# Attention slots: outputs in slots 0 to 3, keys and queries two by two, x turned in slots 5 and 6

## The reference, cut to what matters

```
x = LN(where(vol > 0.5, x + circuit(x), x + gelu(x@w1+b1)@w2+b2))     # per batch, then scale and shift
q, k, v = x@Wq+bq, x@Wk+bk, x@Wv+bv                                   # 16 heads of 32 columns
p   = softmax(q k^T / sqrt(32) + bias[b, head], masked columns -> 0)  # bias is 8x16x512x512
x   = x + (p v)@Wo + bo                                               # attention
out = h + gelu(h@W1+b1)@W2+b2, h = LN(x)*g2+beta2                     # second FFN
```

## Time and profile before

| What | Value |
|---|---|
| median of 3 runs | 2408.28 us (2406.91 to 2420.22) |
| the profiled execution's own time | 2410.64 us |
| its span, first to last instruction | 2408.8 us |
| mean granted TensorE clock | 0.997 |
| first FFN / attention / second FFN | 798.2 / 887.2 / 723.4 us |
| a middle batch of attention | 110.9 to 111.4 us |

### The profile page before, as it was taken

The page is one execution under the profiler, slowest core; times in us unless marked ns, Lnnn a source line. Parts: engine busy times, 40 slices in busy tenths (PEclk is TensorE's granted clock), DMA queues, the critical chain, the costliest instruction groups (busy, mean ns, idle before and its releaser), DMA issues. The chain is left out here.

```text
span 2408.8 us, 42244 instructions
## 1 busy us (share of the span) xinstructions
PE 2368.5 (98%) x16104; PEld 1896.9 (79%) x16104; DVE 1355.8 (56%) x2749; ACT 1010.2 (42%) x2057; POOL 1018.5 (42%) x829
## 2 busy tenths in 40 slices
PE   9999999999999899999999999998999999999999
PEld 7788888888887677777777777776888888888887
DVE  7354454454457777777777777778443333323332
ACT  6132232231332776767666676767311211111111
POOL 0042241431424896767676776767112112202200
PEclk9999999999999999999999999999999999999999
DMA  7110111101123466565656565574420110110100
GB/s 230 45 44 18 44 35 44 44 17 61 44 80 111 148 192 199 158 209 162 201 163 198 168 200 184 173 209 156 131 71 1 52 52 0 52 52 0 52 35 18
DMA packets 142197, 243.94 MB, mean 101 GB/s; under 512 B 14140, under 2 KB 28620, under 8 KB 142048
## 3 DMA queue, kind: packets, MB, share of 16 engines
q1 hardware_dynamic: 140992, 241.40, 31.3%
q10 hardware_dynamic: 1056, 0.52, 0.1%
HBM read 216.69 MB, written 25.20 MB: 100 GB/s over the span
## 5 line engine op out<-in xcount | busy, mean ns | idle before, releaser
L1251 POOL TENSOR_TENSOR at_bias<-at_bias,at_mask 128x512 f32<-128x512 f32 x512 | 592.7, 1186 | 239.2 <-DMA at_bias<-in_fside_Bx16xSxS 226.7
L647 ACT ACTIVATE L_hid<-bank,L_b1c 128x512 f32<-128x512 f32 x256 | 176.6, 690 | 961.6 <-PE bank L290 961.4
L843 DVE CAST L_hh<-L_hid 128x512 fp32r<-128x512 f32 x256 | 121.7, 475 | 743.2 <-PE bank L970 714.5
L288 PE MATMUL bank<-xth,L_w1h 128*128 128x512 f32 x1024 | 402.7, 393 | 0.5 <-DVE L_w1l L714 0.5
L289 PE MATMUL bank<-xth,L_w1l 128*128 128x512 f32 x1024 | 399.5, 390 | 0.0
L290 PE MATMUL bank<-xtl,L_w1h 128*128 128x512 f32 x1024 | 399.4, 390 | 0.0
L968 PE MATMUL bank<-L_w2h,L_hh 128*128 128x512 f32 x1016 | 398.0, 392 | 0.0
L970 PE MATMUL bank<-L_w2l,L_hh 128*128 128x512 f32 x1016 | 395.6, 389 | 0.0
L969 PE MATMUL bank<-L_w2h,L_hl 128*128 128x512 f32 x1016 | 395.4, 389 | 0.0
L1307 ACT ACTIVATE at_bias<-at_bias,cos_sin 128x512 f32<-128x512 f32 x512 | 363.2, 713 | 3.9 <-DVE cos_sin L1448 3.5
L1448 DVE CUSTOM_DVE_ANT_0 at_bias<-bank,at_bias 128x512 f32<-128x512 f32 x512 | 331.6, 683 | 35.0 <-PE bank L1638 23.5
(11 more groups left out here) (213 smaller groups left out, 3242.2 us busy)
## 6 DMA issues: line engine op xcount, KB each, us to landing
at_bias<-in_fside_Bx16xSxS SPq DMA_DIRECT2D x256, 512.0 KB, 3.6
L_ring<-in_L_cond_w SPq DMA_DIRECT2D x32, 256.0 KB, 5.0
L_xres<-in_x SPq DMA_DIRECT2D x8, 1024.0 KB, 5.3
x_scratch<-L_xres SPq DMA_DIRECT2D x8, 1024.0 KB, 4.3
at_xres<-x_scratch SPq DMA_DIRECT2D x32, 256.0 KB, 4.4
L_xin<-x_scratch SPq DMA_DIRECT2D x8, 1024.0 KB, 5.6
L_xres<-x_scratch SPq DMA_DIRECT2D x8, 1024.0 KB, 5.5
L_xin<-in_x SPq DMA_DIRECT2D x7, 1024.0 KB, 5.1
```

Source lines behind the costliest of these rows:

```text
L288: nc_mm = pe.matmul(out, ah, bh, start=i == 0, stop=False)
L647: nc.scalar.activation(hid[m % 2][:, :], turn[m % 2][:, :], func, bias=b1c[:, m:m + 1]).then_inc(h_act, 1)
L1251: nc.gpsimd.tensor_tensor(tile, tile, mask[:, m % TT, :], ALU.add).then_inc(masked, 1)
```

## The change

Only tables and the waits that follow from them change. Outputs 0, 1, 2, 3 lie in slots 0, 1, 2, 3, one each. The queries of tile 1, which lay in slot 0, are made in slot 15 of the batch before, and its keys in slot 14 (in the first batch the queries stay in slot 0). The keys and queries of tile 3 move from 7 and 8 to 6 and 7. The values move from 9, 12, 13, 14 to 8, 9, 12, 13. x is turned two transposes each in slots 5 and 6. Output 0 may start when three head groups of the context are there; its last three matmuls (k = 3) wait for the fourth.

```
-    KEYS = {0: (1, 1), 4: (2, 0), 5: (2, 1), 7: (3, 0), 8: (3, 1), 10: (4, 0), 11: (4, 1), 15: (5, 0)}
-    OUTS = {1: (0,), 2: (1,), 3: (2, 3)}
-    VALUES = {9: 0, 12: 1, 13: 2, 14: 3}
-    TURNS, LAST_TURNS = {6: (0,), 7: (1,), 8: (2, 3)}, {12: 0, 13: 1, 14: 2, 15: 3}
+    KEYS = {4: (2, 0), 5: (2, 1), 6: (3, 0), 7: (3, 1), 10: (4, 0), 11: (4, 1), 14: (5, 0), 15: (5, 1)}
+    FIRST_KEYS = {0: (1, 1), **KEYS}
+    OUTS = {0: 0, 1: 1, 2: 2, 3: 3}
+    VALUES = {8: 0, 9: 1, 12: 2, 13: 3}
+    TURNS, LAST_TURNS = {5: (0, 1), 6: (2, 3)}, {12: 0, 13: 1, 14: 2, 15: 3}
...
                 if m == 0:
-                    nat_hi_of(b, 1, 0, gen)
+                    nat_hi_of(b, 1, 0 if first else 1, gen)
...
                 if before in OUTS and not first:
-                    output(b - 1, OUTS[before][-1], gen)
+                    output(b - 1, OUTS[before], gen)
...
-                if m in OUTS and len(OUTS[m]) == 2 and not first:
-                    output(b - 1, OUTS[m][0], gen)
...
             if i == 0 and steps[0] == 0:
                 pe.wait_ge(w_lo, 4)
+                pe.wait_ge(ct_lo, b * PHASES + PHASES - 1)
+            if i == 0 and steps[-1] == 3 * KT - 1:
                 pe.wait_ge(ct_lo, b * PHASES + PHASES)
...
-            if m in OUTS and m - 1 in OUTS:
-                pe.wait_ge(o_out, b * TT - TT + OUTS[m][0])
+            if m in OUTS and m and not first:
+                pe.wait_ge(o_out, b * TT - TT + OUTS[m])
             elif m in OUTS or (m == 4 and first):
-                pe.wait_ge(nat_lo, nat_count(b, 1, 1))
+                pe.wait_ge(nat_lo, nat_count(b, 1, 0 if m == 0 and first else 1))
             elif m == 4:
                 pe.wait_ge(o_out, b * TT)
-            elif m == 9:
+            elif m == 8:
                 pe.wait_ge(nat_lo, nat_count(b, 3, 1))
-            elif m in (10, 13, 14):
-                pe.wait_ge(v_out, b * TT + TT + (1 if m == 10 else VALUES[m]))
+            elif m in (9, 13):
+                pe.wait_ge(v_out, b * TT + TT + VALUES[m])
+            elif m in (10, 14):
+                pe.wait_ge(v_out, b * TT + TT + VALUES[m - 1] + 1)
             elif m == 12:
                 pe.wait_ge(nat_lo, nat_count(b + 1, 0, 1))
-            elif m == 15:
-                pe.wait_ge(v_out, b * TT + 2 * TT)
...
-                if len(OUTS[m]) == 1:
-                    output(b - 1, OUTS[m][0], some, gen)
-                elif j < 2:
-                    output(b - 1, OUTS[m][0], range(6 * j, 6 * j + 6), gen)
-                elif j == 3:
-                    pe.wait_ge(o_out, b * TT - TT + OUTS[m][1])
-                    output(b - 1, OUTS[m][1], ALL, gen)
+                output(b - 1, OUTS[m], some, gen)
```

More of the change, by code:

```diff
@@ L1359, in body @@
                         turn_hi(b + 1, 1 - odd, k, turn[0])
-                if before in KEYS:
-                    tile, query = KEYS[before]
+                keys = FIRST_KEYS if first else KEYS
+                if before in keys:
+                    tile, query = keys[before]
                     if tile < KT:
@@ L1513, in body @@
                 if m == 0:
-                    nat_lo_of(b, 1, 0, gen)
+                    nat_lo_of(b, 1, 0 if first else 1, gen)
                 if before in OUTS and not first:
-                    output(b - 1, OUTS[before][-1], gen)
+                    output(b - 1, OUTS[before], gen)
                 if after:
@@ L1691, in beside @@
             some = range(3 * j, 3 * j + 3)
-            if m in KEYS and (KEYS[m][0] < KT or not last):
+            keys = FIRST_KEYS if first else KEYS
+            if m in keys and (keys[m][0] < KT or not last):
                 if j == 0:
                     gen_free(b, m, first)
-                tile, query = KEYS[m]
+                tile, query = keys[m]
                 project(odd if tile < KT else 1 - odd, tile % KT, query, some, gen)
```

## The result

| | before | after |
|---|---|---|
| median of the runs (lowest to highest) | 2408.16 us (2404.23 to 2420.22, 9 runs) | 2402.6 us (2400.7 to 2405.25, 9 runs) |
| ratio, with its 95% interval | 1 | 0.9973 [0.9961, 0.9986] |
| profiled execution, its span | 2410.64, 2408.8 us | 2401.96, 2400.2 us |
| mean granted TensorE clock there | 0.997 | 0.998 |

The kernel is 5.6 us (0.23%) faster from median to median (0.27% by the ratio): no change beyond the 0.5% that the prediction drew as its bound, within its range of 2393.5 to 2405.5, and 4.5 us above its middle of 2398.1. The interval excludes 1, so the gain is clear of the noise: the prediction was too cautious where it said that nothing under 0.5% can be told from no change. The forecast gain was 10.2 us, so a bit over half of it came.

A forecast was written before the change was run, and what follows sets the result against it. PE, busy for 98% of the span, was taken to bound the kernel. First batch +0.3, six middle batches -7.4 and last batch -3.1 gave -10.2 us, from the median 2408.3 to 2398.1 us; range 2393.5 to 2405.5.

The forecast's parts named there:

- The bound and the asymmetry: PE busy 98% of the span; slot 3's second projection costs its full 2.95 us, one in gappy slot 6 less.
- The middle batches: Six middle batches of attention: -1.24 us each, -7.4 us together.
- slot 7: Middle batches: 7.57 to 7.02 us, less 0.08 us of wait for DVE's copy behind the spreading: -0.47 us.
- Slot 0's new wait: Output 0's last three matmuls wait for the fourth context block's low part: +0.75 us a batch, bounds 0.68 and 1.75.
- Rival 2: DVE collides with POOL in slot 0, low part 1.81 us in all seven batches: +7.0 us, 2405.1 us; chance 20%.
- A rare collision: Slot 0: 0.07 us a batch allowed for the low part's occasional meeting with POOL's mask adds.
- The first batch: Slot 5 +0.88, slot 6 +2.11, slot 7 -0.47, slot 8 -2.24 us: together +0.3 us.
- The last batch: Slot 0 +0.75, slot 3 -2.95, slot 6 +0.74, slot 7 -1.36, slot 8 -0.3: together -3.1 us, bounds -4.0 and 0.
- it could now come in slot 8 or 9: Last batch: half clock, 1.7 us each time PE is busy throughout, might move there; counted only in the bounds.
- the 0.70: Chance that the changed kernel's time lies within 0.5% of the time before.
- Rival 3: Stalls in slot 0 or slots 5 to 7 bring half clock, two drops per batch: +23.8 us, 2422 us; chance 4%.

The follow-up runs named there:

- turns_alone: Kernel before with only x's turns moved, two blocks each in slots 5 and 6: 2407.2 us, ratio 1.0002.
- few_masks: Changed kernel with GpSimd adding the mask to one of 512 columns of each bias tile: 2392.79 us, ratio 0.9943.
- early_lo: Changed kernel with the last context block's high and low parts made earlier in slot 0: 2400.63 us, ratio 0.9969.
- lo_last: Changed kernel with output 0's one matmul that needs the context's low part put last, alone waiting for it: 2398.97 us, ratio 0.9962.
- both_lo: Changed kernel with early_lo and lo_last together: 2398.63 us, ratio 0.9959.
- before_again: Kernel before, unchanged, run and profiled a second time: 2407.75 us, ratio 0.9999.
- last_old: Changed kernel with tile 3's keys and queries back in slots 7 and 8 of the last batch only: 2400.1 us, ratio 0.9966.
- best: Changed kernel with early_lo, lo_last and last_old together: 2395.54 us, ratio 0.9949.
- fill_last: Changed kernel with 9 and 12 thrown-away matmuls in slots 8 and 9 of the last batch: 2403.19 us, ratio 0.997.
- combo: Changed kernel with lo_last, fill_last and x turned 2, 1, 1 in slots 5, 6, 7 together: 2399.44 us, ratio 0.996.

## Why the prediction was right, and where not

**The bound and the asymmetry: right.** PE bounds the kernel; a second projection in slot 3 cost its full 2.97, and in slot 6 a projection costs 0.96 once x is turned there twice. turns_alone separates the two: the turns alone give nothing, and the even filling gives what the middle batches gain.

**The middle batches: right.** -7.4 forecast, -7.7 from one pair of profiles, -6.2 from the other. Each slot was within 0.1 us in the fourth batch. The one term a little off is slot 7: over the six middle batches it took 7.01 to 7.53, 7.24 in the mean, so it gained 0.33 and not 0.47. The path was the one written down (spreading, then copy, then PE's last turn), but the median spreading (0.70 before) was the wrong measure: PE sees the long ones alone, and few_masks shows that those come from POOL.

**Slot 0's new wait: right,** +0.71 of +0.75 forecast, and removed by early_lo, lo_last and both_lo. Rival 2 happens as well, in none of the batches of one profile and in three of the other's for 1.5 us together. "A rare collision" at 0.07 a batch was somewhat low: over the five profiles with this slot 0 it comes to 0.12 a batch, in nine of 35.

**The first batch: +0.93 for +0.3.** Slot 5 +0.86, slot 6 +2.30 (2.11 forecast), slot 7 -0.23 (-0.47), slot 8 -2.25 (-2.24), and slot 9 +0.25, which the sum held at nothing. Slot 6's excess lies at its head. Its stretch and timeline in the changed kernel, then the same split of Wo in few_masks:

```profile
839.85:847.88 8.03, 7.80 (x82) 6.03 (x82) 6.48 (x14) 6.01 (x14) 7.95 (x8) 1.00 0.41 138
```

```profile
839.00 1.65 DVE L1418 TENSOR_TENSOR at_wol<-at_passing,at_woh 128x512 fp32r<-128x512 f32 x1
...
840.68 0.60 ACT L1291 ACTIVATE at_xth<-bank 128x512 fp32r<-128x512 f32 x1 [1.41 <-DVE at_wol L1418]
```

```profile
833.50 0.68 DVE L1418 TENSOR_TENSOR at_wol<-at_passing,at_woh 128x512 fp32r<-128x512 f32 x1
```

ACT's eviction of x waits for that split, as the prediction said (0.4 us, bounds 0 to 1.66), and beside POOL the split takes 1.65 in the place of 0.68. With the adds nearly gone slots 6, 7 and 9 of this batch take 7.44, 7.00 and 6.57, where the changed kernel has 8.03, 7.35 and 6.82. So the 1.2 us by which the changed kernel's exceed those is POOL's, more than the 0.6 by which the forecast was missed. The sum had paid for POOL in one slot and not in the others.

**The last batch: the step that failed.** "Slot 7 takes 8.56 because the granted clock was 0.50 ... With slot 6 filled I expect it at 7.2: -1.36." The reading of the row was right, and slot 7 did take 7.01. But the slow row was no fixed part of the kernel: with slot 6 as thin as ever it came in two of five profiles, with slot 6 filled in none of nine. That bears out the direction of the term, in few profiles, and not its size: two in five of 1.5 us is 0.6 on average (an estimate), and I took 1.36 off the median. And slot 9, priced at nothing, went from 6.18 to 7.78 (8.10 in the second profile), for two reasons: the projection taken out of slot 8 had been what hid DVE's late low part and copy (0.63), and half clock now falls there (0.86), in all seven profiles of this order without the filling. The prediction had named that risk ("it could now come in slot 8 or 9") and put it into its bounds of -4.0 and 0, not into the sum. I had looked for what covers the work that moves; here the moved work was itself the cover of something. Slot 6 took 7.01, not 6.60 (+1.15 for +0.74). Slot 8 took 7.14 as forecast in the first profile, but 6.79 in the second. Together the last batch came out 0.4 to 0.7 longer than before_again's, with 6.8 and 10.2 us at half clock for its 6.8, where I had -3.1.

**The two sums.** Profile to profile -8.7 us for -10.2 forecast; median to median -5.6. The profiled execution of before had three stretches of half clock in its last batch, and the prediction said that it lay 2.4 us over the median, but treated that as an offset and not as something that its last-batch term would use up. The second pair of profiles, of executions near their medians, gives -4.9 for attention (883.77 to 878.88): first batch +0.9, middle batches -6.2, last batch +0.4. Against the sum's +0.3, -7.4 and -3.1 the last batch is two thirds of the miss. That the time still fell well inside the range owes something to luck: the last batch came out past the upper bound of its own term, 0, when held against before_again.

**The chances.** Below 2396.2 us (faster by over 0.5%) the changed kernel did not come in any run; 2402.6 lies inside the 0.70. Rival 3, half clock by the new stall in slot 0 or by slots 5 to 7, did not show: the middle batches stand at 1.00. Half clock came where the prediction had it only as a bound, in slot 9 of the last batch.

## What to carry to other kernels

When one stage has two of something on the engine that bounds and another stage has none, price the move by what the thin stage lacks there (its gaps), not by the work's length, and test it by moving only what accompanies it. Before taking a row at half clock as part of a kernel, look in how many executions it stands at the same place: here one such row carried 1.36 us of a forecast gain that came out 4.6 us short. And ask of work that leaves a slot what it was covering, and whether it leaves a thin stretch behind; the fastest version keeps the old order in the last batch, though the runs don't settle what that alone gives.

## What the hardware showed that was not expected

**The mean granted clock is not the same from execution to execution of one kernel,** and the time of the kernel before follows it. 65 executions, from three of the comparisons:

| mean granted clock | executions | time, us |
|---|---|---|
| 0.999 | 17 | 2403.9 to 2407.7 |
| 0.998 | 23 | 2405.7 to 2409.3 |
| 0.997 | 20 | 2406.6 to 2414.7 |
| 0.996 | 5 | 2410.8 to 2418.6 |

The changed kernel had 0.996 in 11 of 20 executions, 0.997 in 5, 0.998 in 3 and 0.999 in 1. A stretch as in the earlier trace rows costs half its length, 1.7 us, when PE is busy throughout, and 0.001 of the mean clock over 2408 us is about 1.4 of these. So the change made the kernel meet half clock more often, and the profiles say where: in slot 9 of the last batch, behind a slot 8 in which PE is busy for 4.3 of 7 us. It costs less there: for a step of 0.002 the time moves by 1.2 us in the changed kernel (means of its 11 executions at 0.996 and 3 at 0.998), by 4.1 us in the kernel before (0.997 against 0.999). PE waits in that slot anyway; the first profile gives 0.86 us for it. last_old and best (0.997 to 0.999), fill_last (0.997 to 0.999) and combo (0.998 to 0.999) meet it less, but fill_last gained nothing by it, since its own matmuls took as much.

**A short VectorE instruction can wait for a whole GpSimd add at a place where nothing orders the two.** The spreading of 0.43 us took up to 1.43, the low part of 0.75 up to 1.74, the split of Wo of 0.68 took 1.65, all beside adds of 1.17; where they meet depends on when a bias tile's DMA lands. The end is regular: a low part that met an add ended 0.54 to 0.56 us after the add, a spreading that began within one 0.28 to 0.29 us after it, in every profile. So what such a collision costs is read from the end of the add.
